# First attention of a fused attention and FFN kernel: projection weights loaded in 128-byte pieces, turned by VectorE, their low part made by GpSimd

## What is computed

```
qkv = jnp.einsum('sbh,ph->sbp', tokens, weight_qkv)
...
attn = jax.nn.softmax(scores, axis=-1)
out = jnp.einsum('bhst,bhtd->bhsd', attn, v)
out = out.transpose(2, 0, 1, 3).reshape(S, B, NUM_HEADS * HEAD_DIM)
return jnp.einsum('sbe,he->sbh', out, weight_proj)
```

## Time and profile before

| What | us |
|---|---|
| Median of 3 runs | 1540.57 |
| The profiled execution, its own time | 1550.29 |
| Its span in the trace | 1548.6 |
| First attention, from the start of iteration 1 to the hand-over | about 60 to 283.6 |
| One steady iteration (3 to 7) | 30.72 |
| TensorE busy in the span | 1485.0 (96%) |

### The profile page before, as it was taken

The page is one execution under the profiler, slowest core; times in us unless marked ns, Lnnn a source line. Parts: engine busy times, 40 slices in busy tenths (PEclk is TensorE's granted clock), DMA queues, the critical chain, the costliest instruction groups (busy, mean ns, idle before and its releaser), DMA issues.

```text
span 1548.6 us, 26991 instructions
## 1 busy us (share of the span) xinstructions
PE 1485.0 (96%) x8792; PEld 1269.1 (82%) x8792; DVE 1208.1 (78%) x2700; ACT 866.8 (56%) x2260; POOL 878.9 (57%) x1231
## 2 busy tenths in 40 slices
PE   6699999989999999999999999999999999999997
PEld 4588888778888888888888888888888888888885
DVE  5688887778778887788788888878788888777865
ACT  2322232356666666666666666666666666666641
POOL 1111343256666666766676676667666766676521
PEclk9899999999999999999999999999999999999999
DMA  8988765222212221222122222212221222211102
GB/s 184 230 169 173 171 137 148 80 83 72 79 55 71 69 77 57 72 68 71 57 81 71 69 68 75 71 55 73 80 69 57 74 74 59 88 57 50 41 27 82
DMA packets 169701, 133.37 MB, mean 86 GB/s; under 512 B 119187, under 2 KB 128787, under 8 KB 169563
## 3 DMA queue, kind: packets, MB, share of 16 engines
q1 hardware_dynamic: 152098, 97.56, 23.9%
q0 software_dynamic: 16464, 33.85, 7.4%
q10 hardware_dynamic: 1000, 0.23, 0.1%
HBM read 107.47 MB, written 7.34 MB: 74 GB/s over the span
## 4 chain that ended last, share of the span: by engine, by line
PE 86%; SPq 5%; ACT 2%; issue 2%; DVE 2%; POOL 1%; DMA 1%; POOLq 0%; DVEq 0%
PE ps_t L932 14%; PE ps_o L746 11%; PE ps_o L748 11%; PE ps_o L747 10%; PE ps_b L746 5%; PE ps_b L748 5%; PE ps_b L747 5%; PE ps_q L748 4%; PE ps_q L747 4%; PE ps_q L746 4%; PE ps_a L746 3%; PE ps_a L747 3%; PE ps_a L748 3%; SPq L454 2%; PE ps_a L795 2%
## 5 line engine op out<-in xcount | busy, mean ns | idle before, releaser
L1418 ACT ACTIVATE sm<-sm,mn 128x640 f32<-128x640 f32 x256 | 211.4, 826 | 233.6 <-DVE mn L1908 227.1
L1784 DVE TENSOR_TENSOR pT_lo<-ps_t,pT_hi 128x512 fp32r<-128x512 f32 x320 | 220.2, 688 | 114.5 <-ACT pT_hi L1341 101.5
L629 POOL DMA_INDIRECT kraw<-in_L_cond_k_cache_dram,idx_a x200 | 197.4, 987 | 89.2 <-issue 75.7
L1341 ACT ACTIVATE pT_hi<-ps_t 128x512 fp32r<-128x512 f32 x320 | 188.5, 589 | 85.1 <-PE ps_t L932 82.2
L629 POOL DMA_INDIRECT vraw<-in_L_cond_v_cache_dram,idx_a x200 | 198.6, 993 | 59.6 <-issue 59.3
L932 PE MATMUL ps_t<-ident,sm 128*128 128x128 f32 x1280 | 196.4, 276 | 3.5 <-DVE sm L1920 1.5
L932 PEld LDWEIGHTS ps_t<-ident,sm 128*128 128x128 f32 x1280 | 148.7, 141 | 51.6 <-DVE qT_lo L1784 17.5
L646 POOL TENSOR_TENSOR z<-pairs_p,zl 128x128 f32<-128x128 f32 x160 | 57.9, 402 | 193.6 <-DVE pairs_p L1637 193.6
L746 PE MATMUL ps_o<-wo_lo,oT_hi 128*128 128x512 f32 x256 | 118.0, 461 | 12.4 <-ACT kvown L1345 10.8
L746 PE MATMUL ps_o<-pT_lo,v_hi 128*128 128x512 f32 x320 | 129.8, 405 | 0.0
L748 PE MATMUL ps_o<-pT_hi,v_hi 128*128 128x512 f32 x320 | 125.5, 392 | 0.0
(11 more groups left out here) (257 smaller groups left out, 4305.6 us busy)
## 6 DMA issues: line engine op xcount, KB each, us to landing
fv<-st SPq DMA_DIRECT2D x128, 128.0 KB, 2.4
tab<-tab_scratch SPq DMA_DIRECT2D x64, 256.0 KB
wblk<-n_L_attn_weight_qkv_dram SPq DMA_DIRECT2D x32, 384.0 KB
wpraw<-_L_attn_weight_proj_dram SPq DMA_DIRECT2D x8, 1024.0 KB, 5.6
mask<-mask_scratch SPq DMA_DIRECT2D x64, 128.0 KB
wtile<-in_L_cond_Wq_dram SPq DMA_DIRECT2D x28, 256.0 KB
wtile<-in_L_cond_Wo_dram SPq DMA_DIRECT2D x28, 256.0 KB
kraw<-in_L_cond_k_cache_dram,idx_a POOLq DMA_INDIRECT x200
```

What stands on the lines that cost most here:

```text
L629: pool.indirect_dma_start(raw[:, par, c, :], None, rows_d, bass.IndirectOffsetOnAxis(idx[:, k:k + 1].bitcast(U32), 0)).then_inc(arrived[pa ...
L1341: act.activation(dst, src, ACT.Copy).then_inc(t_hi, 1)
L1418: act.activation(sm[:, h, :], sm[:, h, :], ACT.Exp, bias=mn[:, h:h + 1], scale=-1.0, accum_out=den[:, h:h + 1]).then_inc(e_done, 1)
L1784: dve.tensor_tensor(lo, src, hi.bitcast(F32), ALU.subtract).then_inc(t_lo, 1)
```

## The change

The projection weights take the way of the qkv weights. `load_wp(g)` becomes 16 DMAs, one for each head and each quarter of the partitions, each of 32 partitions x 16 pieces of 128 bytes (64 KB). `p_turn(g, h)` on VectorE transposes 128x512 of `wpblk` into `wpT_turn`. `p_copy` reads that instead of PSUM. `p_low` goes to GpSimd and writes `wpT_lo` over `wpT_turn` (the same place in SBUF). The transposes on TensorE go, and so do their places in the ring. `load_wp(0)` is issued after the adapters instead of ahead of them, and `load_wp(1)` after `load_w(1)` instead of ahead of it.

```diff
-        T_FIRST = ["P0", "P1", "P2", "P3"]
-        T_BOTH = ["Z0", "Z1", "P0", "P1", "Z2", "P2", "P3", "Z3", "Z4"]
+        T_FIRST = []
+        T_BOTH = ["Z0", "Z1", "Z2", "Z3", "Z4"]
...
             def load_wp(g):
-                sp.dma_start(wpraw[g % 2][:], w_proj[:, g * QW:(g + 1) * QW].rearrange("(t p) e -> p t e", p=P)
-                             ).then_inc(wp_in[g % 2], 16)
+                blocks = w_proj[:, g * QW:(g + 1) * QW].rearrange("(k b) (h i a) -> i h b k a", b=32, h=HG, i=4)
+                for h in range(HG):
+                    for i in range(4):
+                        sp.dma_start(wpblk[g % 2][32 * i:32 * i + 32, h, :, :], blocks[i, h]).then_inc(wp_in[g % 2], 16)
 
             load_w(0)
-            load_wp(0)
...
-            load_wp(1)
+            load_wp(0)
             sp.wait_ge(w_turned, 4)
             load_w(1)
+            load_wp(1)
...
+            def p_low(g, h):
+
+                pool.wait_ge(p_hi, HG * g + h + 1)
+                pool.tensor_tensor(wpT_lo[:, h, :], wpT_turn[:, h, :], wpT_hi[:, h, :].bitcast(F32), ALU.subtract
+                                   ).then_inc(p_lo, 1)
...
+            for h in range(HG):
+                p_low(0, h)
             for g in range(G):
                 for s in range(N):
                     z_products(g, s)
+                if g + 1 < G:
+                    for h in range(HG):
+                        p_low(g + 1, h)
...
-                act.wait_ge(p_full, HG * g + h + 1)
-                act.activation(wpT_hi[:, h, :], ring(g, f"P{h}")[:, :], ACT.Copy).then_inc(p_hi, 1)
+                act.wait_ge(p_turned, HG * g + h + 1)
+                act.activation(wpT_hi[:, h, :], wpT_turn[:, h, :], ACT.Copy).then_inc(p_hi, 1)
...
-            def p_low(g, h):
-                dve.wait_ge(p_hi, HG * g + h + 1)
-                dve.tensor_tensor(wpT_lo[:, h, :], ring(g, f"P{h}")[:, :], wpT_hi[:, h, :].bitcast(F32), ALU.subtract
-                                  ).then_inc(p_lo, 1)
+            def p_turn(g, h):
+                if h == 0:
+                    dve.wait_ge(wp_in[g % 2], 256 * (g // 2 + 1))
+                if g >= 1:
+                    dve.wait_ge(fo_full, HG * (g - 1) + h + 1)
+                dve.transpose(wpT_turn[:, h, :], wpblk[g % 2][:, h, :, :].rearrange("p k a -> p (k a)")
+                              ).then_inc(p_turned, 1)
...
             for i in range(1, G):
                 if 1 < i < G - 1:
                     turn(i + 1)
+                p_turn(i, 0)
                 z_low(i, 0)
                 z_low(i, 1)
                 fold_low(i)
-                p_low(i, 0)
+                p_turn(i, 1)
                 x2_sum(i, 0)
```

More of the change, by code:

```diff
@@ L73, in block_program @@
         wpraw = [at("wpraw0", [P, HG, HID], F32, 172), at("wpraw1", [P, HG, HID], F32, 12)]
+        wpblk = [at("wpblk0", [P, HG, 16, 32], F32, 172), at("wpblk1", [P, HG, 16, 32], F32, 12)]
+        wpT_turn = at("wpT_turn", [P, HG, HID], F32, 160)
         wpT_hi = at("wpT_hi", [P, HG, HID], F32R, 20)
@@ L234, in block_program @@
         w_turned = sem("w_turned")
-        p_full = sem("p_full")
+        p_turned = sem("p_turned")
         p_hi = sem("p_hi")
@@ L770, in ring @@
                 return mm
-            def p_group(g, h):
-                if h == 0:
-                    pe.wait_ge(wp_in[g % 2], 16 * (g // 2 + 1))
-                ring(g, f"P{h}", [wpraw[g % 2][:, ot, h * P:(h + 1) * P] for ot in range(NC_)]).then_inc(p_full, 1)
             def z_group(i, j):
@@ L880, in _ @@
             scores_s(0, 1)
-            p_group(0, 3)
             scores_s(0, 2)
@@ L898, in _ @@
                 fold(i, 5)
-                p_group(i, 0)
                 z_out(i, 0)
@@ L902, in _ @@
                 mix_product(i)
-                p_group(i, 1)
                 z_out(i, 2)
@@ L911, in _ @@
                 scores_s(i, 3)
-                p_group(i, 2)
                 fold_out(i, 1)
@@ L916, in _ @@
                 scores_s(i, 5)
-                p_group(i, 3)
                 z_group(i, 3)
@@ L1679, in x2_low @@
                                   x2T_hi[:, :, s, :].bitcast(F32), ALU.subtract).then_inc(x2t_lo, 1)
+            p_turn(0, 0)
+            p_turn(0, 1)
             fold_low(0)
-            p_low(0, 0)
-            p_low(0, 1)
-            p_low(0, 2)
+            p_turn(0, 2)
+            p_turn(0, 3)
             products_s(0, 0)
@@ L1687, in _ @@
             out_low(0, 0)
-            p_low(0, 3)
             sums_s(0, 0)
@@ L1721, in _ @@
                     turn(2, [1])
-                p_low(i, 1)
+                p_turn(i, 2)
                 x2_sum(i, 2)
@@ L1736, in _ @@
                 products_s(i, 3)
-                p_low(i, 2)
+                p_turn(i, 3)
                 sums_s(i, 2)
@@ L1743, in _ @@
                 products_s(i, 5)
-                p_low(i, 3)
                 z_low(i, 3)
```

5 lines of the change are left out of this document (removed).

## The result

The changed kernel takes 1549.31 us (median of 5 runs, 1547.32 to 1549.74) where the kernel before takes 1540.30 (5 runs, 1535.82 to 1542.01) on the same chip: 1.0054 times as long, with a 95% interval of 1.0037 to 1.0071. It is 9.0 us slower. The prediction was 1552.6, between 1541 and 1565.

The account below looks back on a forecast made before the run. DMA issue was taken to bound the start up to 105.6 us, TensorE afterwards. `z_out(3, 0)` 16.0 us late, 0.3 back in three iterations, then 1.77 and 1.3, gave +12.0 us: 1552.6, range 1541 to 1565.

Parts of the forecast that it names:

- The account of SyncE's queue: First attention's start: DMA issues summed in order, 10.15 us per projection load, making the queue 13.9 us late after `scatter(0)`.
- Rival 3: SyncE's projection loads: an issue costs 0.83 us, giving 1571, or 1562 at half of it; chance 0.15.
- 188 GB/s: Rate during one qkv load, taken to show 128-byte pieces slower than 2 KB rows; about 5.6 us for 1 MB.
- the holding of the scatter behind the load: SyncE's steady turns: scatter held 3.1 us behind the qkv load, within a turn of 30.4 us.
- 28.95 of TensorE: Steady iteration where TensorE is the bound: 30.72 less 1.77 us for 16 transposes removed.
- VectorE's exchange: VectorE in each iteration: 32 subtractions go, 32 transposes come; no change, with 5.2 us of slack.
- In iteration 0 they lay before a stretch that VectorE sets: Iteration 0: the removed TensorE transposes stood ahead of a VectorE-bound stretch; no cost was put on it.
- the forecast's own range: Late SyncE queue at the start, then 30 us queue turns in the steady part: 1548 to 1558, chance 0.5.
- rival 2: Start late, but TensorE bounds the steady part as holding shrinks under 1.5 us: +7.6 us, 1541 to 1549, chance 0.22.
- sign of being wrong: SyncE's queue: 16 issues under 8 us, `scatter(0)` ending before 70 us, or gaps ahead of loads in iterations 3 to 5.
- Rival 1: SyncE's issues are hidden and TensorE stays the bound, so 12.4 us come off: 1528 to 1537, chance 0.09.
- Rival 4: The longer chain VectorE, ScalarE, GpSimd makes `fold_out` late: +1 to 3 us on top, chance 0.04.

Follow-up runs that it names:

- e11: The kernel before, unchanged, run and profiled a second time; ratio 0.9991 against itself, median 1540.25 us.
- e12: The changed kernel, unchanged, for its third trace, on the same chip as e11; ratio 1.0047, median 1548.13 us.
- e10: The changed kernel, unchanged, run and profiled a second time beside the kernel before; ratio 1.0049.
- e5: The changed kernel with `p_turn(i, 1)` moved between the two low parts of z, earlier on VectorE; ratio 1.0048 against the kernel before.
- e8: The changed kernel with e4's and e5's edits, plus heads 2 and 3 of groups 2 to 7 issued by ScalarE; ratio 0.9962 against the kernel before.
- e9: e8 with group 0's weights turned ahead of the mask tables on VectorE and copied ahead of ScalarE's `folded`; ratio 0.9995 against the kernel before.
- e7: The changed kernel with the projection weights' low part made on VectorE again instead of GpSimd; ratio 1.0091 against the kernel before.
- e4: The changed kernel with the first 32 projection issues (groups 0 and 1) moved from SyncE to ScalarE; ratio 0.9992 against the kernel before.

## Why the prediction was right, and where it wasn't

The steps of the sum, as they were predicted and as the changed kernel's first trace has them, us:

| step | predicted | measured |
|---|---|---|
| adapters issued | 28.8 | 29.2 |
| `load_wp(0)`, `load_w(1)`, `load_wp(1)` issued | 39.0, 46.0, 57.6 | 38.8, 46.1, 56.6 |
| table stores issued | 66.0 | 65.1 |
| `scatter(0)` issued | 76.2 | 75.2 |
| `turn(2, [0])` | 87.7 | 87.0 |
| iteration 1 ends | 111.5 | 111.7 |
| `scatter(1)` issued, `z_out(2, 0)` | 117.7, 119.5 | 116.3, 118.15 |
| `scatter(2)` issued, `z_out(3, 0)` | 150.6, 152.4 | 147.5, 149.4 |
| a turn of SyncE's queue, steady | 30.4 | 28.3 (then 28.7, 28.1) |
| a steady iteration | 30.4, the last 28.95 | 29.5 |
| the loss at the hand-over | 12.0 | 6.8; 8.5 between e11 and e12 |

**Right: what bounds the start, and by how much.** The account of SyncE's queue, one issue after the other, holds to within 1 us up to the first scatter and carries over to VectorE's turn and to the end of iteration 1. The value taken for an issue, 0.635 us from the row with the same number of partitions, was near the measured 9.55/16 = 0.60. For the same 64 KB the Trainium skill, "DMA: Bandwidth & Descriptors", section Bandwidth, has 0.95 us, taken on another queue and for the moving of the data, not for the issue; that estimate gave 15.2 us a load, and no load here took more than 11.14. Its rule on overhead (section Rules for kernel authors) is for transfers under 64 KB, not up to 64 KB as the prediction has it. Rival 3, which put an issue at 0.83 or half the way there, falls by the same rows: even the load that met a full queue, at 82.38, took 11.14/16 = 0.70. One reading beside the sum was wrong: that 188 GB/s show the pieces to be slower than rows. In the trace of before the one DMA of 1 MB in 2 KB rows lands 5.6 us after its issue, and 1 MB in 5.6 us is the same rate.

**Wrong: the step "the holding of the scatter behind the load".** The prediction put 3.1 us of holding and 10.15 us for the scatter itself into each steady turn, from a row in which the scatter followed a load of 6.98 us directly (13.20 us). The scatter took 11.67 us, 1.6 less. The projection issues took 9.6 instead of 10.15. Together the turn is 28.3 us and not 30.4. It is shorter than an iteration of TensorE, so from iteration 4 on **the queue isn't the bound**, and TensorE gives back its share in every iteration (but for the one wait of 1.12 us in e10). `z_out(3, 0)` is 13.0 us late, not 16.0: the end of `scatter(2)` was put 3.1 us too late, 1.5 of it by `load_wp(3)` (8.61 us instead of 10.15), 0.5 by `scatter(1)` (12.71 instead of 13.20), 0.9 by the queue up to the first scatter.

**Wrong by a small wait: "28.95 of TensorE".** The iterations that are bound by TensorE last 29.5, because of the transpose that stands ahead of `x2_sum(i, 0)` on VectorE. The prediction had put VectorE's exchange, one transpose for one subtraction, at nothing, with 5.2 us of slack. The durations are equal indeed (690 ns and 691), and the slack is there; but what was exchanged doesn't stand at the same place of the chain. e5 shows this: 28.98 with the turn elsewhere. So each iteration gives back 1.2 us instead of 1.77.

**Missing: iteration 0.** "In iteration 0 they lay before a stretch that VectorE sets" had no cost. The chain transposes, copies, low part makes `fold_out` wait 3.7 us, and the fold of iteration 1 starts at 64.06 instead of 60.30 (61.91 in e11). In the changed kernel it is hidden, since VectorE waits 7.6 us for the queue afterwards; once the queue is mended it is there still, as in e8, whose fold starts at 64.07. What it costs by itself wasn't measured, since e9 moved other work too.

**What this makes of the rivals.** The time lies in the forecast's own range, 1548 to 1558, at its lower end, and 0.3 us above that of rival 2 (1541 to 1549), so the time doesn't decide between them; that it fell on the forecast's side is luck. The traces decide: the forecast's mechanism holds for the first half only. The second half is rival 2's, "the start is late, but the steady part has a TensorE bound", and its condition is met or nearly so: the 3.1 us of holding shrank to 1.5 (it named "under 1.5"), and a turn lasts less than 28.95 us. Its sum, +7.6 us, is nearer to the measured differences (9.0, 9.5 and 7.9 by the medians, 6.8 and 8.5 at the hand-over) than my 12.0. The sum of what was measured: +13.1 us at the end of iteration 1 (111.66 against 98.52), 1.8 back in iteration 2, 0.3 more in iteration 3 (its wait of 1.83 is more than it saves), and 1.2 back in each of the last four: 13.1 - 1.8 + 0.3 - 4.9 = 6.8 (from the unrounded rows). The 1.9 us to the 8.7 at the first rotation are the clock's. Between e11 and e12, on one chip, the same sum is 13.04 - 0.35 + 0.64 - 4.84 = 8.5: with the wait of 1.13 us at `z_out(2, 0)` iteration 2 gives back almost nothing, as was predicted. That is the better pair. The first trace of before, on which the prediction and the 6.8 rest, had lost some 2 us itself to a lower clock in iteration 1 (see the last section).

**Signs.** The 16 issues, the first scatter, the first turn of group 2 and the 32 transposes (0.70 us) came as predicted, and no sign of being wrong showed. But TensorE waited about 2 us at `z_out(3, 0)` and not 4, the next three had no wait in two traces of three, and the last iteration took 29.5 us and not 28.95.

Rival 1 (issues hidden) was wrong in the kernel as it is. In e8, where ScalarE issues more than half of them, the sign is its own, but 6.8 us came off and not 12.4: a wait of 3.2 us for `fv`, 5.1 with what the clock adds, and iteration 0 stand in the way. Rival 4 is refuted by e7 for the steady part and true for iteration 0.

**What stays open.** Why the granted clock falls at the hand-over in some traces and not in others, with the same waits ahead of it; and what makes ScalarE's `kvown` late by some 10 us on some chips or executions. Neither depends on this change. What e5's edit is worth in time wasn't measured with an interval that could show 2 us. How far e4 owes its gain to group 0's loads and how far to group 1's wasn't tried.

## What to carry to other kernels

A layout that spares the busiest engine some work has a price in the queue that issues its DMAs: count the issues, multiply by half a microsecond or so, and follow the queue in order to the first transfer that something waits for. Here 32 issues took 20 us at the start and the first scatter came 13 us later, since the issues beside them became shorter; that was more than all later iterations could give back. An engine that idles there can issue them instead, as in e4 and e8. And put no DMA-held work ahead of work that a queue waits for, as e9 did.

When two kernels differ in their first part only, compare the time at which that part ends. The spans of two executions can differ by 10 us in the part that is the same.

## What wasn't expected of the hardware

- An issue on SyncE costs by its form: 16 DMAs of 64 KB take 8.18 to 8.33 us in rows of 2 KB and 9.55 us in pieces of 128 bytes at the same place of the queue, in the steady part 7.55 and 8.6 to 9.6. One DMA of 1 MB takes 0.51 us to issue where the queue is free.
- GpSimd's subtraction of 128x512 floats takes 1.28 us and VectorE's 0.69 with an operand in PSUM, 0.65 without (e7), yet it is the better place: it makes an iteration 0.6 us shorter (e7).
- A wait of TensorE can cost more than its length: 3.24 us in e8 made an iteration 5.1 us longer, with a granted clock of 0.50 for the 3 us behind it. The clock doesn't follow such a wait each time: behind the 2.13 us at `z_out(3, 0)` in e5 it was 1.00 from 149 to 155 us, behind the 2.08 us at the same place in e4 it was 0.56 from 135 to 138.
- The granted clock at the same place in the same kernel was 1.00 in one execution and 0.72 over 12 us in another, and was worth 1.9 us. After the wait of 3.36 us behind `turn(2, [0])` it was 0.76 from 80 to 84 us in the first trace of before; in e11, where that wait was 1.23 us, it stayed at 1.00. TensorE went on at 78.44 and 78.30 us and was at `z_out(2, 0)` at 105.35 and 103.39: 1.8 us that go with the clock, which the prediction had estimated at 1 to 2.
